# Relation products of a typed graph layer as eight 32-row products per tile on compact block-diagonal matrices, with staging and stores by whole tiles

## The chip, the cores and the metric

One core of one Trainium2 chip runs the whole program in one launch. The metric is the device time of the run in microseconds; the figure compared is the median of three runs.

## What is computed

Four graph layers run one after the other on 6250 nodes with 128 features and 100000 edges, each with a residual and a layer norm. The change lies ahead of the third one, a graph transformer with 8 heads of 16 columns, 8 node types and 8 edge types. Cut to what matters:

```python
k = _decomp(node_feat, node_type, w_comp_k, w_basis_k).reshape(n, H, DK)   # H = 8, DK = 16
q = _decomp(node_feat, node_type, w_comp_q, w_basis_q).reshape(n, H, DK)
v = _decomp(node_feat, node_type, w_comp_v, w_basis_v).reshape(n, H, DK)
kt = jnp.einsum('nhi,thij->tnhj', k, relation_att)[edge_type, src]
e = (q[dst] * kt).sum(-1) * relation_pri[edge_type] * scale
...
vt = jnp.einsum('nhi,thij->tnhj', v, relation_msg)[edge_type, src]
```

`_decomp` multiplies each node's features by four basis matrices and adds the four products with coefficients of the node's type. The two products over i are the relation products: for each of 8 edge types and each head, the 16 columns of that head by a 16x16 matrix.

## The kernel before, in words

Everything is float32. The nodes are cut into 49 tiles of 128 (`NT`), in 7 groups (`NG`) of 7 (`GT`). The stage in question makes, for each tile, a table of k and v under every edge type (`t3`, 8 edge types x 128 nodes x 256 columns, 1 MB for a tile), from which the next stage gathers rows by edge. The stage begins and ends at a barrier of all engines. The order of the work is written out by hand: each engine has its own program, `first` and `turn`, and semaphores tie them. Group 0 and group 6 are unrolled, groups 1 to 5 are a loop over a register, so that 35 of the 49 tiles run in the loop.

For tile n the engines do this:

- TensorE transposes the features (`features`, L2475) and ScalarE copies them out (`features_T`, L2529). TensorE multiplies them by the four bases of k, v and q, one 512-column product each (`typed`, L2482). ScalarE takes the first part of each (L2544), and VectorE adds the three others (`sums_of`, L2453).
- TensorE transposes k and v (`raise_kv`, L2490), and ScalarE copies them to SBUF (`lower_kv`, L2535).
- TensorE multiplies k and v by the relation matrices (`rows`, L2498). These are block-diagonal: `rel` is 128 rows by 8 types x 128 columns, and within a type only the 16x16 blocks of the heads are not zero. One call of `rows` makes a piece `z`, four of the eight types: two products of 512 columns (k by `att`, v by `msg`), into two banks of PSUM. There are two pieces a tile, in different banks, 2048 moving columns in all.
- ScalarE copies each piece to a staging buffer (`rows`, L2550; 1024 columns at once), and SyncE stores it, 512 KB, to `t3` (L2425). Seven staging buffers are used in turn.

TensorE's order in a turn is `raise_kv(n)`, `typed(n+1)`, `rows(n, 0)`, `features(n+2)`, `rows(n, 1)`. ScalarE's is `lower_kv(n)`, `typed(n+1)`, `rows(n, 0)`, `features_T(n+2)`, `features(n+3)`, `rows(n, 1)`. The transposed features and the transposed k and v share bank 0 of PSUM, and so `raise_kv` waits for the copy of the features that was started before it:

```python
pe.wait_ge(xt_sb, n + 1 + ahead_by)    # in raise_kv: features_T(n+1) has been copied out
need(pe, kv_out, 2 * n + z - 1)        # in rows: the same piece of the tile before is copied out
```

Of the kernel before, what the change touches and what calls it, by code (L numbers as in the profile page):

```python
# [9 lines left out]
ALU = mybir.AluOpType  # L10
ACT = mybir.ActivationFunctionType
# [80 lines left out]
def build(nc, t, out):  # L92
    ctx = ExitStack()
    with ctx:
# [662 lines left out]
        TYPED_AT = NODE_C_AT + NT * 4 * NB  # L757
        basis = {n: arena[:, o:o + NB * D] for n, o in (("a", 0), ("k", TYPED_AT), ("q", TYPED_AT + NB * D), ("v", TYPED_AT + 2 * NB * D))}
        REL_AT = TYPED_AT + 3 * NB * D
        rel = {n: arena[:, REL_AT + i * TN * D:REL_AT + (i + 1) * TN * D] for i, n in enumerate(("att", "msg"))}  # L760
        FREE_AT = REL_AT + 2 * TN * D
        acc_att = arena[:, AT_ACC:AT_ACC + NT * (D + H)]
        acc_gcn = arena[:, AT_ACC:AT_ACC + NP]
# [1002 lines left out]
        def attention_pass(which, idx, table, width, keep, tab, tab_w, head_last, Nodes=None):  # L1766
# [102 lines left out]
            with nc.Block() as block:  # L1869
# [7 lines left out]
                @block.sync  # L1877
                def _(sp):
                    def lows(n, k, b):
                        need(sp, oT_hot, n - 1)  # L1880
                        sp.dma_start(lo_b[:, b, :], lo_rows[bass.ds(n, 1), :].to_broadcast([P, 8 * P])).then_inc(lo_in[b], 16)

                    def reload(n, k, r):

                        b = r % 2
                        need(sp, mm, 2 * n - 2)
                        sp.wait_ge(spilled[r], 16 * k + 16)
                        sp.dma_start(m[:, b, :, 0:D], spill[bass.ds(n, 1)].rearrange("o p (c f) -> p (o c) f", f=D)).then_inc(back_in[b], 16)

                    def weights():  # L1890

                        for n in "akqv":
                            sp.dma_start(basis[n].rearrange("p (b o) -> p b o", b=NB), t["L2_gnn_w_basis_" + n].rearrange("b (i o) -> i b o", o=D)).then_inc(wt_in, 16)
                        for m, n in enumerate("kvqa"):
                            sp.dma_start(comp[:, :, m, :], t["L2_gnn_w_comp_" + n].partition_broadcast(P)).then_inc(wt_in, 16)
                        sp.dma_start(pri, t["L2_gnn_relation_pri"].rearrange("t h -> (t h)").partition_broadcast(P)).then_inc(wt_in, 16)
                        sp.wait_ge(wt_zero, 4)
                        sp.dma_start(nt_rows[0:NT - 1, :], t["node_type_8"][0:(NT - 1) * P].rearrange("(t p) -> t p", p=P)).then_inc(wt_in, 16)
                        sp.dma_start(nt_rows[NT - 1:NT, 0:LAST], t["node_type_8"][(NT - 1) * P:N].unsqueeze(0)).then_inc(wt_in, 16)
                        for n in ("att", "msg"):  # L1900
                            for h in range(H):
                                sp.dma_start(rel[n][h * DK:(h + 1) * DK, :].rearrange("p (t o) -> p t o", t=TN)[:, :, h * DK:(h + 1) * DK],
                                             t["L2_gnn_relation_" + n][:, h].rearrange("t i j -> i t j")).then_inc(wt_blk, 16)
# [228 lines left out]
                def _(dve):  # L2132
# [40 lines left out]
                    def priorities():  # L2173
                        step = Chain(dve, wt_v, 3 * TN)
                        dve.wait_ge(wt_blk, 16 * 2 * H)
                        step(nc.vector.tensor_scalar(pri, pri, DK ** -0.5, None, ALU.mult))
                        att = rel["att"].rearrange("p (c j) -> p c j", j=DK)
                        step(nc.vector.tensor_tensor(att, att, bcast_last(pri, DK), ALU.mult))

                    def messages(v, j, b):  # L2180

# [207 lines left out]
        new_stage()  # L2389
        x_rdy, xt_ps, xt_sb = (sem("n3_" + n) for n in ("x", "xtps", "xtsb"))  # L2390
        c_set, parts_ps, based, summed, kv_up, kv_sb, kv_ps, kv_out = (sem("n3_" + n) for n in ("cset", "parts", "based", "summed", "kvup", "kvsb", "kvps", "kvout"))
        kv_dma = [sem(f"n3_dma{i}") for i in range(GT)]
        x_new, xT = (scratch(AT_BUF + i * GC, GC) for i in range(1, 3))
        kv_T = scratch(AT_BUF + 3 * GC, 2 * GC).rearrange("p (t a n) -> p t a n", t=GT, a=2)
        KV_AT = FREE_AT
        kv_st = [scratch(AT_BUF + 5 * GC if i == 0 else KV_AT + (i - 1) * 1024, 1024).rearrange("p (t f) -> p t f", f=2 * D) for i in range(GT)]
        kvq = scratch(AT_BUF + 5 * GC + 1024, GT * 3 * D).rearrange("p (t m f) -> p t m f", t=GT, m=3)
        c_st = scratch(AT_BUF + 5 * GC + 1024 + GT * 3 * D, GT * 4 * NB)
        assert AT_BUF + 5 * GC + 1024 + GT * 3 * D + GT * 4 * NB <= EDGES_AT and KV_AT + (GT - 1) * 1024 <= 12800
        t3_rows = t3.rearrange("(t n) f -> n t f", t=TN)  # L2400
        PIECES = 2 * GT
        SUMS = 3 * (NB - 1)
        raised_ps, features_ps = ps[:, 0:2 * P], ps[:, 2 * P:3 * P]

        def part_bank(m):
            return (5 + m) * 512

        def piece_banks(z):
            return ps[:, (1 + 2 * z) * 512:(3 + 2 * z) * 512].rearrange("p (a c) -> p a c", a=2)

        def of_node(i, m, b):
            at_c = 4 * NB * i + NB * m + b
# [4 lines left out]
        with nc.Block() as block:  # L2417
            @block.sync
            def _(sp):
                def body(k):  # L2420
                    for i, number in enumerate(numbers(sp, GT * k, GT)):
                        for z in range(2):
                            n = PIECES * k + 2 * i + z
                            sp.wait_ge(kv_out, n + 1)
                            sp.dma_start(t3_rows[bass.ds(P * number, P), 4 * z:4 * z + 4, :], kv_st[(2 * i + z) % GT]).then_inc(kv_dma[(2 * i + z) % GT], 16)  # L2425
                turns(sp, NG, body)
                for i in range(GT):
                    sp.wait_ge(kv_dma[i], 16 * 2 * NG)

            @block.gpsimd  # L2430
            def _(pool):
# [37 lines left out]
            def _(pe):  # L2469
# [20 lines left out]
                        last = nc.tensor.transpose(raised_ps[:, m * P:(m + 1) * P], kvq[:, i, m], ident[:, :])  # L2490
                    last.then_inc(kv_up, 1)

                def rows(k, i, z):
                    n = GT * k + i
                    pe.wait_ge(kv_sb, n + 1)
                    need(pe, kv_out, 2 * n + z - 1)
                    for a, name in enumerate(("att", "msg")):
                        last = nc.tensor.matmul(piece_banks(z)[:, a, :], kv_T[:, i, a], rel[name][:, z * 512:(z + 1) * 512], start=True, stop=True)  # L2498
                    last.then_inc(kv_ps, 1)

                def first(k):
                    features(k, 0)
# [3 lines left out]
                def turn(k, more):  # L2506
                    for i in range(GT):
                        raise_kv(k, i, 1 if more or i + 1 < GT else 0)
                        if more or i + 1 < GT:
                            typed(*tile_at(k, i + 1))  # L2510
                        rows(k, i, 0)
                        if more or i + 2 < GT:
                            features(*tile_at(k, i + 2))
                        rows(k, i, 1)
                ahead(pe, first, turn)

            @block.scalar
            def _(act):
# [12 lines left out]
                def lower_kv(k, i):  # L2531
                    n = GT * k + i
                    act.wait_ge(kv_up, n + 1)
                    need(act, kv_ps, 2 * (n - GT) + 2)
                    nc.scalar.activation(kv_T[:, i], raised_ps.rearrange("p (a n) -> p a n", a=2), ACT.Copy).then_inc(kv_sb, 1)  # L2535

                def typed(k, i):
# [5 lines left out]
                        act.wait_ge(parts_ps, 3 * n + m + 1)  # L2543
                        nc.scalar.activation(kvq[:, i, m], ps[:, part_bank(m):part_bank(m) + D], ACT.Copy, scale=of_node(i, m, 0)).then_inc(based, 1)  # L2544

                def rows(k, i, z):
                    p = 2 * i + z
                    act.wait_ge(kv_ps, PIECES * k + p + 1)
                    need(act, kv_dma[p % GT], 16 * (2 * k + p // GT))
                    nc.scalar.activation(kv_st[p % GT].rearrange("p t (a f) -> p a t f", a=2),  # L2550
                                         piece_banks(z).rearrange("p a (t f) -> p a t f", f=D), ACT.Copy).then_inc(kv_out, 1)

                def first(k):
                    features(k, 0)
# [6 lines left out]
                def turn(k, more):  # L2561
                    for i in range(GT):
                        lower_kv(k, i)
                        if more or i + 1 < GT:
                            typed(*tile_at(k, i + 1))
                        rows(k, i, 0)
                        if more or i + 2 < GT:
                            features_T(*tile_at(k, i + 2))
                        if more or i + 3 < GT:
                            features(*tile_at(k, i + 3))  # L2570
                        rows(k, i, 1)
                ahead(act, first, turn)

        attention_pass("hgt", d_typed, t3, 2 * D, D, q_tab, D, False)
# [450 lines left out]
```

## Time and profile before

| | before |
|---|---|
| median of 3 runs | 9756.16 us (9746.25 to 9768.41) |
| span of the profiled execution | 7728.3 us |
| TensorE busy | 5090.6 us, 66% |
| VectorE busy | 4789.3 us, 62% |
| ScalarE busy | 3333.2 us, 43% |
| GpSimd busy | 4957.0 us, 64% |
| mean granted TensorE clock | 0.773 |
| the stage in question | about 4762 to 5084 us of the span |

The profile was taken in one execution. Its span goes from the first to the last instruction; of this execution only the span is given, and the median of the runs is 2027.9 us longer than it. A time in the trace is counted from the start of the span. "PEclk" is the granted clock of TensorE as a share of the full 2.4 GHz. A float32 product of TensorE stands in the trace as two weight loads and two products ("MATMUL"), a transpose as one.

### The profile page before, as it was taken

The numbers are of one execution on the slowest core, as the hardware profiler recorded it, in microseconds if no ns is written. First come the engines' busy times: TensorE is split into PE (matmuls) and PEld (weight loads), VectorE is DVE, ScalarE is ACT, GpSimd is POOL, SyncE is SP. The second block draws the span as 40 slices with busy tenths as digits, with TensorE's granted clock in tenths as the row PEclk, the third lists the DMA queues.
The fourth block names the chain that finished last, engine by engine and source line by source line (L and its number), as shares of the span: only waits on it lengthen the run. The fifth ranks groups of instructions, "written<-read, shape, count | busy, mean of one in ns | idle before, by whom it ended". The sixth has DMA issues, their size and how long they took to land. (4 is left out here: it accounts for less than half of the span.)

```text
span 7728.3 us, 120435 instructions
## 1 busy us (share of the span) xinstructions
PE 5090.6 (66%) x26514; PEld 3820.1 (49%) x26515; DVE 4789.3 (62%) x13170; ACT 3333.2 (43%) x8012; POOL 4957.0 (64%) x4968
## 2 busy tenths in 40 slices
PE   8777775666675777772555556956666565777674
PEld 6655653444444555551444444435555543555453
DVE  8766665555554677774566665436666565665666
ACT  0222221444444455540444445536666542555553
POOL 0677775777776777774777770057777601777774
PEclk9655566888887888885666667977777787999997
DMA  0222221111213112123666664467777812666665
GB/s 27 62 54 53 55 52 49 53 55 55 54 54 47 53 54 55 54 54 86 181 176 179 178 174 99 164 182 226 223 225 228 207 58 103 199 198 200 198 199 141
DMA packets 818131, 920.95 MB, mean 119 GB/s; under 512 B 120930, under 2 KB 657002, under 8 KB 817706
## 3 DMA queue, kind: packets, MB, share of 16 engines
q0 software_dynamic: 198144, 441.54, 22.0%
q1 hardware_dynamic: 395902, 365.44, 15.8%
q10 hardware_dynamic: 223916, 112.15, 5.0%
q8 instruction: 54, 0.88, 0.0%
q14 instruction: 115, 0.94, 0.0%
HBM read 724.85 MB, written 193.87 MB: 119 GB/s over the span
## 5 line engine op out<-in xcount | busy, mean ns | idle before, releaser
L788 POOL DMA_INDIRECT arena<-t,stage_idx x3328 | 3288.2, 988 | 1484.5 <-issue 989.7
L827 PE MATMUL ps<-arena 128*128 128x128 f32 (+2 forms) x8320 | 1786.1, 375 | 768.6 <-DMA arena<-t,stage_idx 624.0
L827 PEld LDWEIGHTS ps<-arena 128*128 128x128 f32 x8320 | 1569.0, 256 | 1033.1 <-issue 938.2
L836 DVE TENSOR_TENSOR arena<-arena,ps 128x512 f32 (+2 forms) x1040 | 834.9, 803 | 668.9 <-PE ps L827 610.8
L744 POOL DMA_INDIRECT d_rec<-arena x784 | 787.8, 1005 | 440.6 <-issue 242.3
L2832 POOL DMA_INDIRECT arena<-t,stage_idx x832 | 841.6, 1012 | 296.8 <-issue 222.1
L824 PE MATMUL ps<-int_tmp 128*128 128x512 bf16 (+1 forms) x1664 | 549.9, 399 | 601.8 <-DVE arena L836 327.6
L1279 PE MATMUL ps<-arena 128*128 128x416 f16 x3328 | 736.3, 373 | 0.0
L2042 PE MATMUL ps<-arena 128*128 x2496 | 393.3, 293 | 435.8 <-ACT arena L1930 248.7
L1211 ACT ACTIVATE arena<-arena 128x128 f16<-128x128 f16 x1664 | 662.2, 480 | 6.9
L2042 PEld LDWEIGHTS ps<-arena 128*128 128x128 f32 (+1 forms) x2496 | 343.5, 201 | 496.1 <-issue 473.5
L1938 ACT ACTIVATE arena<-iota_row,stage_lw 128x128 f32<-128x128 f32 x1664 | 508.7, 388 | 6.8
L824 PEld LDWEIGHTS ps<-int_tmp 128*128 128x128 bf16 x1664 | 149.3, 110 | 726.5 <-DVE arena L836 405.9
L1236 DVE TENSOR_SCALAR arena<-iota_row,stage_lw 128x128 f32<-128x128 f32 x1664 | 474.9, 365 | 53.5 <-DVE stage_lw L1228 49.2
L705 PE MATMUL ps<-arena 128*128 128x49 f32 x1568 | 328.0, 391 | 249.7 <-DVE arena L596 249.4
L705 PEld LDWEIGHTS ps<-arena 128*128 128x128 f32 x1568 | 319.8, 310 | 291.1 <-issue 224.6
L2865 ACT ACTIVATE arena<-iota_row,small 128x128 f32<-128x128 f32 x832 | 254.6, 388 | 466.0 <-PE ps L827 465.7
L1279 PEld LDWEIGHTS ps<-arena 128*128 128x128 f16 x3328 | 322.3, 110 | 228.9 <-issue 77.0
L2929 DVE TENSOR_TENSOR arena<-ps,arena 128x512 f32<-128x512 f32 x208 | 143.8, 692 | 452.2 <-DMA arena<-t,stage_idx 394.2
L2294 DVE TENSOR_TENSOR arena<-ps,arena 128x512 f32<-128x512 f32 x208 | 135.6, 687 | 333.6 <-DMA arena<-t,stage_idx 287.1
L1247 DVE TENSOR_SCALAR arena<-arena 128x832 f16<-128x832 f16 x832 | 316.9, 441 | 0.0
L2194 DVE TENSOR_TENSOR arena<-arena 128x512 f32<-128x512 f32 x416 | 268.3, 686 | 39.6 <-DMA arena<-spill 35.0
(466 smaller groups left out, 8299.9 us busy)
## 6 DMA issues: line engine op xcount, KB each, us to landing
spill<-arena ACTq DMA_DIRECT2D x208, 512.0 KB, 4.2
arena<-spill SPq DMA_DIRECT2D x208, 512.0 KB
arena<-t,stage_idx POOLq DMA_INDIRECT x4160, 3.2
arena<-d_loT SPq DMA_DIRECT2D x208, 256.0 KB
arena<-s_loT SPq DMA_DIRECT2D x104, 512.0 KB, 4.2
arena<-key_d SPq DMA_DIRECT2D x98, 512.0 KB
t<-arena SPq DMA_DIRECT2D x98, 512.0 KB, 2.9
d_rec<-arena POOLq DMA_INDIRECT x784
```

Of the source, the lines that this page charges most:

```text
L705: last = nc.tensor.matmul(pick_bank(b)[:, i * NT:(i + 1) * NT], at_loT[:, b, i * EC:(i + 1) * EC], run, start=True, stop=True)
L744: pool.indirect_dma_start(out=d_rec[:, :], out_offset=bass.IndirectOffsetOnAxis(ap=row[:, 8 * b + i:8 * b + i + 1], axis=0), in_=recs_st[: ...
L788: pool.indirect_dma_start(out=rows[r][:, i, :], out_offset=None, in_=table, in_offset=bass.IndirectOffsetOnAxis(ap=stage_idx[:, 8 * r + i: ...
L824: nc.tensor.matmul(half[:, :, 0:self.width], zeros16[:, 0:P], self.blank, start=True, stop=False, skip_group_check=True)
L827: return nc.tensor.matmul(self.banks[i // 4][:, bass.ds(self.slot[i], self.width)], weights, rows, start=False, stop=False, skip_group_che ...
L836: nc.vector.tensor_tensor(at, at, got, ALU.add).then_inc(self.added, 1)
L1211: last = nc.scalar.activation(at_r[:, b, a, j], far[:, b, j], ACT.Relu, bias=place_st[:, b, 2 + 2 * a, j:j + 1], scale=place_st[:, b, 3 + ...
L1236: one_hot = nc.vector.tensor_scalar(at[:, s, :], iota_row[:, :], lw_st[:, s, 0:1], lw_st[:, s, 1:2], ALU.is_equal, ALU.mult)
L1279: nc.tensor.matmul(place_bank(a, z), at_r[:, b, a, j], at_q[:, b, j, z * Q_W:(z + 1) * Q_W], start=False, stop=False, skip_group_check=True)
L1938: last = nc.scalar.activation(at[:, b, i], iota_row[:, :], ACT.Abs, bias=minus_lo[:, 8 * b + i:8 * b + i + 1])
L2042: last = nc.tensor.matmul(looked_up(b, z)[:, (i - 4 * z) * tab_w:(i - 4 * z + 1) * tab_w], hot_T[:, b, i * P:(i + 1) * P], source[:, bass. ...
L2832: pool.indirect_dma_start(out=rows[:, i, :], out_offset=None, in_=t4, in_offset=bass.IndirectOffsetOnAxis(ap=stage_idx[:, i:i + 1], axis=0 ...
```

## The change

The relation matrices are kept compact. Heads 2g and 2g+1 lie in the 32 partitions of group g, and for each type only the 32 columns of these two heads are kept, so `rel` is 128 rows by 8 types x 32 columns. A tile's products are now eight: for k, then for v, and for each of four groups of 32 partitions, the 32 rows of that group by 256 columns. Each group writes a bank of its own, k in one half and v in the other. ScalarE copies group by group, 512 columns each, into a staging buffer that holds a whole tile (three of them, 1 MB each, chosen by (k + i) mod 3), and SyncE stores a whole tile with one transfer. `features` and `features_T` now come behind the whole of `rows`.

```diff
-        rel = {n: arena[:, REL_AT + i * TN * D:REL_AT + (i + 1) * TN * D] for i, n in enumerate(("att", "msg"))}
+        GROUPS_OF = P // 32
+        REL_W = TN * 32
+        rel = {n: arena[:, REL_AT + i * REL_W:REL_AT + (i + 1) * REL_W] for i, n in enumerate(("att", "msg"))}
...
-                        att = rel["att"].rearrange("p (c j) -> p c j", j=DK)
-                        step(nc.vector.tensor_tensor(att, att, bcast_last(pri, DK), ALU.mult))
+                        two = 32 // DK
+                        for g in range(GROUPS_OF):
+                            of_g = slice(32 * g, 32 * g + 32)
...
+                            step(nc.vector.tensor_tensor(att, att, bcast_last(pri_g, DK), ALU.mult))
...
+        STAGES = 3
...
+        def kv_st(k, i):
+
+            return arena[:, bass.ds(KV_AT + ST_W * ((k + i) % STAGES), ST_W)].rearrange("p (t f) -> p t f", f=2 * D)
...
-                        for z in range(2):
-                            n = PIECES * k + 2 * i + z
-                            sp.wait_ge(kv_out, n + 1)
-                            sp.dma_start(t3_rows[bass.ds(P * number, P), 4 * z:4 * z + 4, :], kv_st[(2 * i + z) % GT]).then_inc(kv_dma[(2 * i + z) % GT], 16)
+                        sp.wait_ge(kv_out, GROUPS_OF * (GT * k + i + 1))
+                        sp.dma_start(t3_rows[bass.ds(P * number, P), :, :], kv_st(k, i)).then_inc(kv_dma[i], 16)
...
-                def rows(k, i, z):
+                def rows(k, i):
                     n = GT * k + i
                     pe.wait_ge(kv_sb, n + 1)
-                    need(pe, kv_out, 2 * n + z - 1)
+                    need(pe, kv_out, GROUPS_OF * n)
                     for a, name in enumerate(("att", "msg")):
-                        last = nc.tensor.matmul(piece_banks(z)[:, a, :], kv_T[:, i, a], rel[name][:, z * 512:(z + 1) * 512], start=True, stop=True)
-                    last.then_inc(kv_ps, 1)
+                        for g in range(GROUPS_OF):
+                            of_g = slice(32 * g, 32 * g + 32)
+                            last = nc.tensor.matmul(group_bank(g)[:, a, :], kv_T[of_g, i, a], rel[name][of_g, :], start=True, stop=True)
+                            if a == 1:
+                                last.then_inc(kv_ps, 1)
...
-                        rows(k, i, 0)
+                        rows(k, i)
                         if more or i + 2 < GT:
                             features(*tile_at(k, i + 2))
-                        rows(k, i, 1)
...
-                def rows(k, i, z):
-                    p = 2 * i + z
-                    act.wait_ge(kv_ps, PIECES * k + p + 1)
-                    need(act, kv_dma[p % GT], 16 * (2 * k + p // GT))
-                    nc.scalar.activation(kv_st[p % GT].rearrange("p t (a f) -> p a t f", a=2),
-                                         piece_banks(z).rearrange("p a (t f) -> p a t f", f=D), ACT.Copy).then_inc(kv_out, 1)
+                def rows(k, i):
+                    n = GT * k + i
+                    need(act, kv_dma[(i - STAGES) % GT], 16 * (k + (i >= STAGES)))
+                    for g in range(GROUPS_OF):
+                        act.wait_ge(kv_ps, GROUPS_OF * n + g + 1)
+                        of_g = kv_st(k, i).rearrange("p t (a g f) -> p a t g f", a=2, g=GROUPS_OF)[:, :, :, g, :]
+                        nc.scalar.activation(of_g, group_bank(g).rearrange("p a (t f) -> p a t f", t=TN), ACT.Copy).then_inc(kv_out, 1)
...
-                        rows(k, i, 0)
+                        rows(k, i)
                         if more or i + 2 < GT:
                             features_T(*tile_at(k, i + 2))
                         if more or i + 3 < GT:
                             features(*tile_at(k, i + 3))
-                        rows(k, i, 1)
```

How the instructions of TensorE stand in group 0 of the stage, one tile and the start of the next, before (L2490 is `raise_kv`, L2482 `typed`, L2498 `rows`, L2475 `features`):

```order
L2490 MATMUL ps<-ident,arena 128x128 x2
L2482 MATMUL ps<-arena 128x512 x3
L2498 MATMUL ps<-arena 128x512 x2
L2475 MATMUL ps<-ident,arena 128x128
L2498 MATMUL ps<-arena 128x512 x2
L2490 MATMUL ps<-ident,arena 128x128 x2
L2482 MATMUL ps<-arena 128x512 x3
```

And now (L2499 is `raise_kv`, L2491 `typed`, L2509 `rows`, L2484 `features`):

```order
L2499 MATMUL ps<-ident,arena 128x128 x2
L2491 MATMUL ps<-arena 128x512 x3
L2509 MATMUL ps<-arena 128x256 x8
L2484 MATMUL ps<-ident,arena 128x128
L2499 MATMUL ps<-ident,arena 128x128 x2
L2491 MATMUL ps<-arena 128x512 x3
```

The four 512-column products have become eight of 256 columns in one run, and the transpose of the features has moved from between the two pieces to behind all eight.

ScalarE in the unrolled group 0 before, one tile (L2535 is `lower_kv`, L2544 `typed`, L2550 `rows`, L2529 `features_T`, L2523 `features`):

```order
L2535 ACTIVATE arena<-ps 128x256
L2544 ACTIVATE arena<-ps,arena 128x128 x3
L2550 ACTIVATE arena<-ps 128x2x4x128
L2529 ACTIVATE arena<-ps 128x128
L2523 ACTIVATE arena<-x_cur 128x128
L2550 ACTIVATE arena<-ps 128x2x4x128
```

And now, in the loop, the end of one tile (L2563 is `rows`, L2540 `features_T`, L2534 `features`, L2546 `lower_kv`; "ISA" and "REGISTER_ALU" work out addresses and counts in registers):

```order
L2561 REGISTER_ALU
L2563 ISA
L2563 ACTIVATE arena<-ps 128x2x8x32
L2538 REGISTER_ALU
L80 ISA
L2540 ACTIVATE arena<-ps 128x128
L80 ISA
L2534 ISA
L2534 ACTIVATE arena<-x_cur 128x128
L80 ISA
L2546 ACTIVATE arena<-ps 128x256
```

`features_T`, which stood between the two copies of a tile, now stands behind the last of four, and each of these has register work of its own ahead of it.

## Rows read from the trace of the kernel before

**Rows 1.** The page: span, and busy time of the engines.
```profile
span 7728.3 us, 120435 instructions
PE 5090.6 (66%) x26514; PEld 3820.1 (49%) x26515; DVE 4789.3 (62%) x13170; ACT 3333.2 (43%) x8012; POOL 4957.0 (64%) x4968
```
**Rows 2.** Windows in the stage: busy of PE, PEld, DVE, ACT, POOL; PEclk, DMA share, GB/s.
```profile
4800.00:4850.00 50.00, 50.00 (x135) 22.84 (x134) 24.39 (x79) 29.07 (x64) 0.00 (x0) 1.00 0.48 169
4950.00:5000.00 50.00, 50.00 (x136) 22.88 (x135) 24.48 (x79) 29.06 (x64) 0.00 (x0) 1.00 0.46 164
```
**Rows 3.** Groups of instructions by form, 4775 to 5080 us.
```profile
L2498 PE MATMUL ps<-arena 128*128 128x512 f32 x387 | 179.3, 593 | 1.2 <-ACT arena L2535 1.2
L2550 ACT ACTIVATE arena<-ps 128x1024 f32<-128x1024 f32 x98 | 100.3, 1023 | 89.5 <-PE ps L2498 89.5
```
**Rows 4.** Timeline of one tile in the loop: start, us, engine, line, operation, idle before.
```profile
4901.61 0.35 DVE L2453 SCALAR_TENSOR_TENSOR arena<-ps,arena 128x128 f32 x1 [0.21 <-DVE arena L2453]
...
4902.03 0.27 ACT L2529 ACTIVATE arena<-ps 128x128 f32<-128x128 f32 x1
4902.35 0.14 PEld L2490 LDWEIGHTS ps<-ident,arena 128*128 128x128 f32 x1 [0.28 <-ACT arena L2529]
...
4902.94 1.02 ACT L2550 ACTIVATE arena<-ps 128x1024 f32<-128x1024 f32 x1 [0.44 <-PE ps L2498]
4902.95 2.74 PE L2482 MATMUL ps<-arena 128*128 128x512 f32 x6
...
4903.85 0.38 ACT L2535 ACTIVATE arena<-ps 128x256 f32<-128x256 f32 x1
...
4904.59 3.15 DVE L2453 SCALAR_TENSOR_TENSOR arena<-ps,arena 128x128 f32<-128x128 f32 x8 [2.08 <-ACT arena L2544]
...
4905.53 1.88 PE L2498 MATMUL ps<-arena 128*128 128x512 f32 x4
...
4907.53 1.02 ACT L2550 ACTIVATE arena<-ps 128x1024 f32<-128x1024 f32 x1 [1.43 <-PE ps L2498]
...
4909.30 2.74 PE L2482 MATMUL ps<-arena 128*128 128x512 f32 x6
```
**Rows 5.** Timeline: the first tile, where TensorE started from idle.
```profile
4763.95 5.26 PE L2482 MATMUL ps<-arena 128*128 128x512 f32 x6
...
4769.40 0.44 PE L2490 MATMUL ps<-ident,arena 128*128 128x128 f32 x2 [0.18 <-DVE arena L2453]
4769.68 0.59 PE L2482 MATMUL ps<-arena 128*128 128x512 f32 x1
```
**Rows 6.** Timeline of TensorE in a later stage, full products and one-row products.
```profile
6491.15 1.72 PE L915 MATMUL ps<-l_T,arena 128*128 128x128 f32 x14
6492.71 1.73 PE L915 MATMUL ps<-w_sb,arena 128*128 128x128 f32 x14
6494.36 1.82 PE L2689 MATMUL ps<-bias_sb,ones 1*128 1x128 f32 x14
```
**Rows 7.** ScalarE's 512-column copies out of PSUM in other stages.
```profile
L1962 ACT ACTIVATE arena<-ps 128x512 f32<-128x512 f32 x26 | 15.6, 598 | 116.0 <-PE ps L2029 116.0
```
**Rows 8.** The stage's end: the last copy and the next stage's first transfer.
```profile
5079.11 1.02 ACT L2550 ACTIVATE arena<-ps 128x1024 f32<-128x1024 f32 x1 [0.69 <-PE ps L2498]
5084.30 0.37 SPq L1881 DMA_DIRECT2D arena<-d_loT  x1
```
**Rows 9.** The clears and the scaling of the relation matrices, each by its line.
```profile
L2149 DVE MEMSET arena<- x1: 912/912/912, 3565.0 to 3565.0; 128x1024 f32 x1
L2178 DVE TENSOR_TENSOR arena<-arena x1: 1224/1224/1224, 3661.4 to 3661.4; 128x1024 f32<-128x1024 f32 x1
```
**Rows 10.** Windows of a later stage: PE busy, PEclk, DMA share, GB/s.
```profile
6332.00:6336.00 4.00, 2.15 (x5) 1.00 0.00 0
6344.00:6348.00 4.00, 1.80 (x15) 1.00 0.00 0
6348.00:6352.00 4.00, 0.00 (x0) 0.67 0.80 291
```

More of the change, by code:

```diff
@@ L1901, in weights @@
                             for h in range(H):
-                                sp.dma_start(rel[n][h * DK:(h + 1) * DK, :].rearrange("p (t o) -> p t o", t=TN)[:, :, h * DK:(h + 1) * DK],
+                                lane = h * DK % 32
+                                sp.dma_start(rel[n][h * DK:(h + 1) * DK, :].rearrange("p (t o) -> p t o", t=TN)[:, :, lane:lane + DK],
                                              t["L2_gnn_relation_" + n][:, h].rearrange("t i j -> i t j")).then_inc(wt_blk, 16)
@@ L2176, in priorities @@
                         step(nc.vector.tensor_scalar(pri, pri, DK ** -0.5, None, ALU.mult))
-                        att = rel["att"].rearrange("p (c j) -> p c j", j=DK)
-                        step(nc.vector.tensor_tensor(att, att, bcast_last(pri, DK), ALU.mult))
+                        two = 32 // DK
+                        for g in range(GROUPS_OF):
+                            of_g = slice(32 * g, 32 * g + 32)
+                            att = rel["att"][of_g].rearrange("p (t q j) -> p t q j", t=TN, j=DK)
+                            pri_g = pri[of_g].rearrange("p (t h) -> p t h", h=H)[:, :, two * g:two * g + two]
+                            step(nc.vector.tensor_tensor(att, att, bcast_last(pri_g, DK), ALU.mult))
                     def messages(v, j, b):
@@ L2395, in build, with group_bank @@
         KV_AT = FREE_AT
[L2396 to L2399, printed above, removed]
+        ST_W = TN * 2 * D
+        kvq = scratch(AT_BUF + 5 * GC, GT * 3 * D).rearrange("p (t m f) -> p t m f", t=GT, m=3)
+        c_st = scratch(AT_BUF + 5 * GC + GT * 3 * D, GT * 4 * NB)
+        assert AT_BUF + 5 * GC + GT * 3 * D + GT * 4 * NB <= EDGES_AT and KV_AT + STAGES * ST_W <= 12800 and GT % STAGES == 1
         t3_rows = t3.rearrange("(t n) f -> n t f", t=TN)
-        PIECES = 2 * GT
         SUMS = 3 * (NB - 1)
         raised_ps, features_ps = ps[:, 0:2 * P], ps[:, 2 * P:3 * P]
+        def kv_st(k, i):
+            return arena[:, bass.ds(KV_AT + ST_W * ((k + i) % STAGES), ST_W)].rearrange("p (t f) -> p t f", f=2 * D)
         def part_bank(m):
             return (5 + m) * 512
-        def piece_banks(z):
-            return ps[:, (1 + 2 * z) * 512:(3 + 2 * z) * 512].rearrange("p (a c) -> p a c", a=2)
+        def group_bank(g):
+            return ps[:, (1 + g) * 512:(2 + g) * 512].rearrange("p (a c) -> p a c", a=2)
         def of_node(i, m, b):
@@ L2421, in body @@
                     for i, number in enumerate(numbers(sp, GT * k, GT)):
-                        for z in range(2):
-                            n = PIECES * k + 2 * i + z
-                            sp.wait_ge(kv_out, n + 1)
-                            sp.dma_start(t3_rows[bass.ds(P * number, P), 4 * z:4 * z + 4, :], kv_st[(2 * i + z) % GT]).then_inc(kv_dma[(2 * i + z) % GT], 16)
+                        sp.wait_ge(kv_out, GROUPS_OF * (GT * k + i + 1))
+                        sp.dma_start(t3_rows[bass.ds(P * number, P), :, :], kv_st(k, i)).then_inc(kv_dma[i], 16)
                 turns(sp, NG, body)
                 for i in range(GT):
-                    sp.wait_ge(kv_dma[i], 16 * 2 * NG)
+                    sp.wait_ge(kv_dma[i], 16 * NG)
             @block.gpsimd
@@ L2533, in lower_kv @@
                     act.wait_ge(kv_up, n + 1)
-                    need(act, kv_ps, 2 * (n - GT) + 2)
+                    need(act, kv_ps, GROUPS_OF * (n - GT) + GROUPS_OF)
                     nc.scalar.activation(kv_T[:, i], raised_ps.rearrange("p (a n) -> p a n", a=2), ACT.Copy).then_inc(kv_sb, 1)
```

## The prediction

> **What bounds the kernel now.** I read the page first: no engine is busy for more than 66% of the span [rows 1], so nothing is to be read from the average, and the change touches one stage of some 310 us between two barriers. So I went to the windows of that stage. There TensorE is busy all the time, 50.00 of 50.00 us, at granted clock 1.00, with ScalarE at 29 and VectorE at 24 of 50, and the DMA engines at a share below 0.5 [rows 2]. Before the change TensorE sets the stage's pace. The groups say what ends ScalarE's waits: it waits 89.5 us for the relation products, and these wait 1.2 us for it [rows 3]. The timeline of one tile shows the period. The typed products start at 4902.95 and again at 4909.30: 6.35 us a tile [rows 4]. In it, the six records of the typed products take 4905.53 - 4902.95 = 2.58 us, 0.43 us a record of 512 columns (1.2 GHz would double that: six took 5.26 us in the first tile [rows 5]). The relation products are eight such records, 3.44 us; transposes fill the rest.
>
> **What the change does to this.** Moving columns stay at 2048 a tile: sixteen records of 256 columns, 0.43 / 2 = 0.215 us each, 3.44 us if they follow one another. A saving can only come from products of different partition groups running at the same time. What the change certainly does is in the order. `raise_kv(n+1)` waits for `features_T(n+2)`, which ScalarE now starts only behind all four copies of tile n. Before, that copy stood between the two pieces, and TensorE still had the second piece to do: the copy starts at 4902.03 and the weight load of `raise_kv` follows at 4902.35, behind running products [rows 4]. Now TensorE has nothing left. The period becomes a closed chain through both engines:
>
> 1. from the start of `raise_kv` to the first typed product, TensorE idle before: 4769.68 - 4769.40 = 0.28 us [rows 5];
> 2. the typed products: 2.58 us [rows 4];
> 3. the change from 128-row to 32-row products. Fourteen full products take 6492.71 - 6491.15 = 1.56 us, and the next fourteen, followed by one-row products, 6494.36 - 6492.71 = 1.65 us [rows 6]: 0.09 us;
> 4. relation products until group 0 of v is through, then the signal. In the trace ScalarE starts 4907.53 - 4905.53 = 2.00 us behind the first of four records, that is 4 x 0.43 + 0.28 [rows 4]. The first copy can start when the tenth record is through;
> 5. four copies of 512 columns. One lasts 598 ns [rows 7]; the next instruction starts 0.11 us before one ends (1.02 us for L2550 at 4902.94, L2535 at 4903.85 [rows 4]), so 0.49 us each, 1.96 us;
> 6. from the start of `features_T` to `raise_kv`: 4902.35 - 4902.03 = 0.32 us [rows 4];
> 7. in the loop the address of the copy is worked out behind the wait. VectorE's last sum, whose address is dynamic too, starts 0.21 us behind the one before [rows 4], where sums with fixed addresses stand about 0.04 apart (eight of 0.35 us in 3.15 us). I take 0.17 us once a tile; for the other copies it lies beside the copy before.
>
> Item 4 is the unknown. No row shows products of different 32-row groups side by side. **Upper bound:** no overlap: 10 x 0.215 + 0.28 = 2.43 us. **Lower bound:** the four groups run wholly together, and a round costs one product, 0.43 us: 2 x 0.43 + 0.28 = 1.14 us. In between: the two records of one product use the same rows and can't overlap, and records start in order; so the first record of group g+1 goes beside the second of group g, a new product starts every 0.215 us, and the tenth record is through after 6 x 0.215: 1.29 + 0.28 = 1.57 us. I take this one, since the records of a float32 product come in pairs and the code issues group behind group.
>
> Period with fixed addresses: 0.28 + 2.58 + 0.09 + 1.57 + 1.96 + 0.32 = 6.80 us, in the loop 6.97 us. Against 6.35 that is 0.45 us for 13 of the 48 periods and 0.62 us for 35: 5.9 + 21.7 = **+27.6 us**. TensorE's work falls to about 5 us a tile and is then idle for almost 2, waiting for ScalarE.
>
> The Trainium skill, TensorEngine Tiling (Array Packing), PSUM Bottleneck, says that packing speeds up TensorE but not the copies out of PSUM, which may become the bottleneck; and TensorE: Matmul & The Clock Gate, Part 3, gives a measured 3.07x for four row tiles of 512 columns. As an estimate by that figure the relation products take 3.44 / 3.07 = 1.12 us, item 4 becomes 1.40 us, and the sum +19 us in place of +27.6. No trace here shows that figure.
>
> The small edits: the stores carry the same bytes, a whole tile every 7 us into three buffers. A buffer is needed again some 18 us later; now seven half-size stores are in the ring and ScalarE never waits for one, and from the last copy (ends 5080.13) to the next stage's first transfer it is 4.17 us with 512 KB [rows 8]. That tail may grow by 1.5 us with 1 MB, or not at all if the engines share it better. One end less: group-wise copies let the last tile finish about 1 us earlier. The two clears of the relation matrices shrink from 912 ns to a quarter, 1.4 us less at the start of a stage; the scaling, 1224 ns, becomes four pieces [rows 9], about the same. I take -1 us for all, bounds -3 and +3. Sum: **+27 us**.
>
> **Profile and median.** The sum is made in the profiled execution, whose span is 7728.3 us; the median of the runs is 2027.9 us longer [rows 1]. No row says what fills that; I take it as the same before and after, so 9756 + 27 = 9783 us. Were it spread over the program, 27 would become 34. I count 0.2%, 19.5 us, as what a measurement of this kernel can tell from no change.
>
> **The rivals.**
>
> *No overlap of the groups.* Item 4 is 2.43 us, the period 7.66 and 7.83, and 13 x 1.31 + 35 x 1.48 - 1 = +68 us: 9824 us. For it: every product in the trace is paced by its columns, one behind the other. Against: the groups use different rows and different banks.
>
> *Full overlap.* Item 4 is 1.14 us, 0.43 us less: 27 - 48 x 0.43 = +6 us, 9762 us, no change that can be told. For it: the order k for all groups, then v for all, leaves each group free for three products. Against: the paired records. This is the case that the skill's Part 3, named above, speaks for; the Trainium skill's figure would put it at +19.
>
> *The clock falls.* TensorE is now idle for 2 of every 7 us. At 1.2 GHz the chain would be about 0.45 + 5.16 + 0.09 + 2.86 + 0.17 + 1.96 + 0.32 = 11.0 us, +223 us if all periods were so; a quarter of them gives about +80. For it: the clock falls to 0.67 in a window without work. Against: it stays at 1.00 through windows with 2.15 and 1.80 of 4 us [rows 10], and at 1.2 GHz TensorE would be busy again for 9 of 11 us. 9830 to 9980 us.
>
> *Faster.* The other side needs TensorE to be the slower party. If in the timed runs the clock of this stage were lower than the 1.00 of the profile, the work taken from TensorE would weigh more: before, a tile costs 6.35 / f; after, about 4.15 / f + 2.82. They cross at f = 0.78. At f = 0.5 it is 12.7 against 11.1, 49 x 1.6 = 78 us less: 9680 us. For it: the unexplained 2 ms between span and median, and the mean clock of 0.773. Against: [rows 2] at 1.00.
>
> **How the numbers follow.** Half overlap 0.49 (9772 to 9800, of which some 0.06 lies below the 0.2% line), no overlap 0.21 (9810 to 9845), full overlap 0.12, falling clock 0.08, faster 0.10. Faster by over 0.2%: 0.10. Within 0.2%: 0.12 + 0.06 = 0.18. Slower: 0.43 + 0.21 + 0.08 = 0.72. The likeliest is 9783 us, its own range 9772 to 9800. The range for 8 in 10 leaves out faster (0.10) and most of the falling clock (0.08): 9755 to 9855 us.
>
> **What would show it.** In the windows of the stage TensorE's busy time falls from 50 to some 36 to 40 of 50 at clock 1.00. In the timeline the typed products start every 6.8 to 7.0 us; `raise_kv` (L2499) has about 1.9 us of idle ahead of it, ended by `features_T` (L2540). The relation products (L2509) show starts 0.1 to 0.12 us apart if they overlap by half, 0.215 if not. The four copies (L2563) last about 0.6 us each, back to back. I would be wrong if `raise_kv` found `features_T` done, if the copies of 32-column runs took another time than plain ones, or if a copy waited for a store.

## The result, and the profile after

The changed kernel takes 9793.73 us (median of 5 runs, 9782.37 to 9812.03) against 9757.12 us before (5 runs, 9746.25 to 9773.53): a ratio of 1.0037, 95% interval 1.0025 to 1.0049, or 24 to 48 us slower. The forecast was 9783.

The page after shows a span that does not answer to [rows 1]: 9780.5 us against 7728.3. The kernel before had been timed in executions of some 9757 us and profiled in one of some 7730 us, and the experiments show that it has both speeds. So the spans can't be compared here, only the stage itself.

```profile
span 9780.5 us, 121265 instructions
PE 5352.0 (55%) x26906; PEld 3939.9 (40%) x26907; DVE 4755.0 (49%) x13173; ACT 3321.8 (34%) x8110; POOL 4953.1 (51%) x4968
```

Windows of the stage after, to be set beside [rows 2] (busy of PE, PEld, DVE, ACT, POOL; PEclk, DMA share, GB/s):

```profile
6290.00:6340.00 50.00, 33.39 (x193) 16.16 (x192) 23.78 (x76) 28.51 (x73) 0.00 (x0) 0.97 0.45 157
6340.00:6390.00 50.00, 33.22 (x175) 15.95 (x175) 22.45 (x72) 28.25 (x73) 0.00 (x0) 0.93 0.42 147
```

TensorE's busy time has fallen from 50 to 33 us of 50, so products of different groups ran side by side. ScalarE still has 28 to 29. And the granted clock is no longer 1.00.

The timeline of one tile after, to be set beside [rows 4]:

```profile
6399.99 2.23 DVE L2462 SCALAR_TENSOR_TENSOR arena<-ps,arena 128x128 f32<-128x128 f32 x6
6400.22 0.74 PEld L2509 LDWEIGHTS ps<-arena 32*128 32x128 f32 x16 [0.76 <-issue]
6400.22 1.15 PE L2509 MATMUL ps<-arena 32*128 32x256 f32 x16
6400.33 0.37 ACT L2555 ACTIVATE arena<-ps,arena 128x128 f32<-128x128 f32 x1 [0.49 <-PE ps L2491]
6401.30 0.14 PEld L2484 LDWEIGHTS ps<-ident,arena 128*128 128x128 f32 x1 [0.33 <-issue]
6401.30 0.33 PE L2484 MATMUL ps<-ident,arena 128*128 128x128 f32 x1
6401.54 2.06 ACT L2563 ACTIVATE arena<-ps 128x512 f32 x4 [0.85 <-PE ps L2509]
...
6403.47 0.31 ACT L2540 ACTIVATE arena<-ps 128x128 f32<-128x128 f32 x1
...
6403.89 0.20 PEld L2499 LDWEIGHTS ps<-ident,arena 128*128 128x128 f32 x2 [2.46 <-issue]
6403.92 0.41 PE L2499 MATMUL ps<-ident,arena 128*128 128x128 f32 x2 [2.29 <-ACT arena L2540]
...
6404.17 2.74 PE L2491 MATMUL ps<-arena 128*128 128x512 f32 x6
...
6406.84 1.15 PE L2509 MATMUL ps<-arena 32*128 32x256 f32 x16
```

Read it as a round. The sixteen records of the relation products start at 6400.22 and take 1.15 us, where eight of 512 columns took 3.44. ScalarE's four copies start at 6401.54, its copy of the features at 6403.47, `raise_kv` at 6403.89, the typed products at 6404.17, and the next relation products at 6406.84: 6.62 us a tile, against 6.35. `raise_kv` has 2.29 us of idle ahead of it, ended by L2540. Over the whole stage, too, most of the idle time ahead of `raise_kv` is ended by this copy:

```profile
L2499 PE MATMUL ps<-ident,arena x98: 272/299/477, 6238.7 to 6565.6; 128*128 128x128 f32 x98
...
  ACT arena L2540: 129.5, 57
```

From the first load of features to the next stage's first transfer it is 6576.80 - 6231.66 = 345.1 us, before 5084.30 - 4762.41 = 321.9 us: 23.2 us more. The first loads, before and after:

```profile
4762.41 0.51 ACT L2523 ACTIVATE arena<-x_cur 128x128 f32<-128x128 f32 x2 [3.15 <-PEq L107]
```
```profile
6231.66 0.51 ACT L2534 ACTIVATE arena<-x_cur 128x128 f32<-128x128 f32 x2 [3.16 <-PEq L107]
```

And the stage's end, beside [rows 8]:

```profile
6568.90 2.06 ACT L2563 ACTIVATE arena<-ps 128x512 f32<-128x512 f32 x4 [1.28 <-PE ps L2509]
6576.80 0.85 SPq L1883 DMA_DIRECT2D arena<-d_loT  x2
```

The last copy ends at 6570.96, and the barrier opens 5.84 us later; before it was 4.17.

### The profile page after: what moved, and what is told of

It reads as the page before. It is cut to its first block and busy times, and to the rows that moved or that the text cites. A ratio compares the mean times of both kernels' runs of the same rounds, so it can differ in the third digit from the quotient of the medians.

```text
span 9780.5 us, 121265 instructions
## 1 busy us (share of the span) xinstructions
PE 5352.0 (55%) x26906; PEld 3939.9 (40%) x26907; DVE 4755.0 (49%) x13173; ACT 3321.8 (34%) x8110; POOL 4953.1 (51%) x4968
## 5 line engine op out<-in xcount | busy, mean ns | idle before, releaser
L829 PE MATMUL ps<-arena 128*128 128x128 f32 (+2 forms) x8320 | 1851.4, 378 | 351.0 <-issue 279.8
L829 PEld LDWEIGHTS ps<-arena 128*128 128x128 f32 x8320 | 1630.2, 259 | 593.5 <-issue 483.0
L826 PE MATMUL ps<-int_tmp 128*128 128x512 bf16 (+1 forms) x1664 | 589.6, 424 | 1336.2 <-issue 692.3
L1281 PE MATMUL ps<-arena 128*128 128x416 f16 x3328 | 846.1, 382 | 540.8 <-issue 539.3
L2045 PE MATMUL ps<-arena 128*128 x2496 | 396.0, 299 | 510.0 <-issue 167.2
L705 PEld LDWEIGHTS ps<-arena 128*128 128x128 f32 x1568 | 334.9, 324 | 521.3 <-issue 519.4
L2940 DVE TENSOR_TENSOR arena<-ps,arena 128x512 f32<-128x512 f32 x208 | 143.3, 689 | 474.1 <-DMA arena<-t,stage_idx 261.1
L2894 PE MATMUL ps<-arena 128*128 x1664 | 278.1, 323 | 136.6 <-issue 135.7
L2894 PEld LDWEIGHTS ps<-arena 128*128 128x128 f32 x1664 | 258.1, 233 | 172.5 <-issue 167.9
L577 ACT ACTIVATE arena<-arena 128x392 bf16<-128x392 bf16 x98 | 89.8, 916 | 648.7 <-DVE arena L342 420.8
```

The costliest lines, as they stand in the source:

```text
L705: last = nc.tensor.matmul(pick_bank(b)[:, i * NT:(i + 1) * NT], at_loT[:, b, i * EC:(i + 1) * EC], run, start=True, stop=True)
L826: nc.tensor.matmul(half[:, :, 0:self.width], zeros16[:, 0:P], self.blank, start=True, stop=False, skip_group_check=True)
L829: return nc.tensor.matmul(self.banks[i // 4][:, bass.ds(self.slot[i], self.width)], weights, rows, start=False, stop=False, skip_group_che ...
L1281: nc.tensor.matmul(place_bank(a, z), at_r[:, b, a, j], at_q[:, b, j, z * Q_W:(z + 1) * Q_W], start=False, stop=False, skip_group_check=True)
L2045: last = nc.tensor.matmul(looked_up(b, z)[:, (i - 4 * z) * tab_w:(i - 4 * z + 1) * tab_w], hot_T[:, b, i * P:(i + 1) * P], source[:, bass. ...
L2894: last = nc.tensor.matmul(ps[:, o_ps:o_ps + D], hot_T[:, b, i * P:(i + 1) * P], p_tab[:, bass.ds(tiles[i] * D, D)], start=True, stop=True)
```

## The experiments

Eleven kernels were run in three batches, each beside the kernel before on one chip. Below, "stage" is the time from the start of the first relation product to the start of the last in the profile: 306.1 us before, 326.8 us in the changed kernel.

```profile
L2498 PE MATMUL ps<-arena x392: 592/592/697, 4772.4 to 5078.5; 128*128 128x512 f32 x196
```
```profile
L2509 PE MATMUL ps<-arena x784: 374/374/479, 6241.6 to 6568.4; 32*128 32x256 f32 x196
```

**The kernel before, again.**

> The kernel before, unchanged, under a new name. It gives a second profile of it, since the first has a span 2027.9 us shorter than its runs while the profile after has a span of 9780.5 us. If something in that one trace was left out, this span comes out near 9755 us and the stage again at 322 us (4762.4 to 5084.3 before); if the kernel really has two speeds, it may come out near 7730 us again. The ratio should be 1.000 within 0.2%.

Median 7745.57 us, ratio 1.0002 (0.9992 to 1.0012), span 7743.7, stage 306.1 us. So the kernel has two speeds: here it takes 7745 us, in the third batch 7744, in the second 9650, and beside the runs of the result it took 9757. Within a batch it keeps to one of them (9609 to 9665 us in 21 runs of the second). Nothing was left out of the first trace; the guess of a gap in it was wrong. The second batch and the third both ran on a chip with the number 7, so the runs don't show that the speed belongs to the chip. The windows of the first graph stage show where the time differs, here first in this run, then in the result's profile of the changed kernel, whose work there is the same:

```profile
1700.00:2000.00 300.00, 202.53 (x1113) 152.36 (x1112) 168.78 (x542) 140.38 (x392) 228.38 (x236) 0.83 0.22 54
```
```profile
1700.00:2000.00 300.00, 158.32 (x836) 105.42 (x836) 123.22 (x403) 104.73 (x292) 186.29 (x187) 0.69 0.15 43
```

GpSimd issues 236 gathers in 300 us at one speed and 187 at the other, and the DMA engines move 54 and 43 GB/s. All stages that gather or scatter are longer in the slower launches. Why was not tried. The stage of this change has the same length in the changed kernel at both speeds (345.1, 343.4 and 345.1 us from end to end at spans of 9780.5, 9665.9 and 7746.5). Of the kernel before there are traces at the faster speed only, 321.9 and 322.0 us.

**The features back between the copies.**

```diff
-                        rows(k, i)
+                        rows(k, i, (0, 1))
                         if more or i + 2 < GT:
                             features_T(*tile_at(k, i + 2))
                         if more or i + 3 < GT:
                             features(*tile_at(k, i + 3))
+                        rows(k, i, (2, 3))
```

> The changed kernel, but ScalarE copies the transposed features (and loads the next ones) between the second and third of its four copies, where the place was before; nothing else moves. Theory A (the chain through features_T sets the pace): raise_kv can start two copies, 0.97 us, earlier in every tile, the period falls from 6.62 us (6.86 with the stretches at the lower clock) to about 5.65 us, and the run is some 45 to 60 us faster than the changed kernel, 15 to 25 us faster than before. Rival B (the four smaller copies themselves, or their register work, set the pace of ScalarE): ScalarE has the same work, so nothing moves, within 10 us of the changed kernel.

7698.49 us, ratio 0.9939 (0.9922 to 0.9955) to before, 47 us faster; the stage is 267.9 us, 58.9 less than in the changed kernel. ScalarE's work is the same, so theory B falls. The expectation from the periods, 45 to 60 less than the changed kernel, held for the stage: two copies, 0.97 us, in 47 periods are 45.6 us, and the clock, which no longer falls, gives the other 13 (see the run with TensorE kept busy). Against before it is more than the 15 to 25 that I gave.

```profile
4850.00:4900.00 50.00, 38.99 (x225) 18.83 (x225) 27.82 (x90) 33.50 (x90) 0.00 (x0) 1.00 0.53 186
```

The clock is back at 1.00, with 39 us of work in 50 and 1.3 us of idle ahead of `raise_kv`.

**The features ahead of the products.** The diff shows TensorE's turn; on ScalarE `features_T` and `features` move ahead of `rows` in the same way.

```diff
-                        rows(k, i)
                         if more or i + 2 < GT:
                             features(*tile_at(k, i + 2))
+                        rows(k, i)
```

> The changed kernel, but the transpose of the features stands ahead of the eight products on TensorE and its copy ahead of the four copies on ScalarE. Theory A: the chain through the copies is cut; the next bound is the round through ScalarE's typed copies and VectorE's sums, about 4.8 to 5.0 us a tile, so some 85 to 100 us faster than the changed kernel and 50 to 70 us faster than before. Rival B: no change beyond 10 us.

7666.4 us, ratio 0.9897 (0.988 to 0.9914), 79 us faster than before, where I had expected 50 to 70; stage 229.5 us, 4.78 us a tile on the mean. The run at the end of this section repeats it beside the changed kernel.

```profile
4903.81 2.06 ACT L2563 ACTIVATE arena<-ps 128x512 f32 x4 [0.57 <-PE ps L2509]
4904.44 0.43 PE L2499 MATMUL ps<-ident,arena 128*128 128x128 f32 x2 [0.80 <-DVE arena L2462]
...
4905.73 0.42 ACT L2546 ACTIVATE arena<-ps 128x256 f32<-128x256 f32 x1
4905.99 0.41 ACT L2555 ACTIVATE arena<-ps,arena 128x128 f32<-128x128 f32 x1
```

`raise_kv` no longer waits for ScalarE's copies: it starts beside them, when VectorE's sums are done. But the copies still hold something up. The first typed copy (L2555), from which the next sums begin, comes right behind them.

**The order alone, in the kernel before**, on TensorE as shown and on ScalarE in the same way.

```diff
                         rows(k, i, 0)
+                        rows(k, i, 1)
                         if more or i + 2 < GT:
                             features(*tile_at(k, i + 2))
-                        rows(k, i, 1)
```

> The kernel before, with the full 512-column products and two pieces, but the transpose of the features and its copy moved behind the second piece, as the change has them. It prices this part alone. Theory A: period 0.28 + 2.58 + 3.44 + 0.28 + 0.91 + 0.42 = 7.91 us against 6.35, so 75 us slower than before, up to 90 if the clock falls in the gaps. Rival B (the products alone set the pace, and the place of the transpose costs nothing): 0 to +10 us.

7810.94 us, ratio 1.0087 (1.0071 to 1.0104), 66 us slower, where theory A had 75; stage 374.2 us, clock 1.00. The period is 7.79 us, where it had 7.91:

```profile
4901.41 2.74 PE L2482 MATMUL ps<-arena 128*128 128x512 f32 x6
...
4903.99 3.60 PE L2498 MATMUL ps<-arena 128*128 128x512 f32 x8
...
4907.62 1.02 ACT L2550 ACTIVATE arena<-ps 128x1024 f32<-128x1024 f32 x1 [0.69 <-PE ps L2498]
4908.54 0.27 ACT L2529 ACTIVATE arena<-ps 128x128 f32<-128x128 f32 x1
...
4908.96 0.41 PE L2490 MATMUL ps<-ident,arena 128*128 128x128 f32 x2 [1.26 <-ACT arena L2529]
4909.20 1.02 PE L2482 MATMUL ps<-arena 128*128 128x512 f32 x2
```

Nothing of the products has changed here, only the place of one transpose, its copy and the load behind it, and TensorE now waits for ScalarE. This is the part of the change that costs.

**The changed kernel, again, in the second batch.**

> The changed kernel, unchanged, under a new name, beside the kernel before on one chip. The times differ by a quarter between chips (9757 us and 7745 us for the kernel before), so the change is to be priced where the other kernels were. The two traces so far, from two chips, show a period of 6.62 us with the clock at 1.00 and 6.86 on the mean against 6.35 before, and a stage of 345.1 us against 321.9. If the stage is all there is to it, this run is 20 to 27 us slower than before on this chip too; if the 36 us measured on the slower chip come from elsewhere too, 30 us or more.

9667.72 us against 9649.57, ratio 1.0024 (1.0014 to 1.0034), 23 us slower (14 to 33) by the ratio, 18 by the medians, where 20 to 27 was expected; stage 325.1 us.

**No overlap.** All products on 128 rows: `kv_T[:, i, a]` and `rel[name]` in place of `kv_T[of_g, i, a]` and `rel[name][of_g, :]`.

> The changed kernel with all eight products on 128 rows (each then sums over all four groups, so the table holds other values): same columns, same banks, same copies, but no product can run beside another. Theory: the relation products take 3.44 us in place of 1.15, the first copy starts after 10 x 0.215 + 0.28 = 2.43 us in place of 1.32 us, the period is 7.6 us, 38 to 53 us slower than the changed kernel by periods (1.1 less the clock's 0.24 us at best). Rival: if the copies hide the products, nothing changes.

9725.64 us, ratio 1.0084 (1.0067 to 1.01). The stage is 369.1 us, 44 more than in the changed kernel beside it, within the 38 to 53 expected; the medians differ by 58. The products take three times as long:

```profile
6303.32 3.62 PE L2509 MATMUL ps<-arena 128*128 128x256 f32 x16
...
6305.84 2.06 ACT L2563 ACTIVATE arena<-ps 128x512 f32 x4 [1.95 <-PE ps L2509]
```

**TensorE kept busy.** Behind the eight products of each tile:

```diff
+                    for _ in range(6):
+                        nc.tensor.matmul(ps[:, 3 * P:4 * P], kv_T[:, i, 0], rel["att"][:, 0:P], start=True, stop=True)
```

> The changed kernel with six more products a tile (128 columns of the compact matrix into an unused part of bank 0, never read) behind the eight, in TensorE's idle stretch of 2.3 us, which they shorten to about 1 us. Theory: the mean period of 6.86 us against 6.62 at full clock comes from stretches in which the granted clock falls because of this idle time; with it shortened the windows of the stage read 1.00 and the run is 5 to 12 us faster than the changed kernel in spite of more work. Rival: the clock's dips have another cause, and it is the same within 3 us or slower.

9654.48 us against 9667.72 for the changed kernel. The ratios to before, 1.0017 (1.0003 to 1.0031) and 1.0024 (1.0014 to 1.0034), overlap, so the run times don't settle it. The stage does: 313.4 us against 325.1, and the clock is 1.00 in every window read.

```profile
6300.00:6350.00 50.00, 43.81 (x289) 26.23 (x288) 24.50 (x78) 29.27 (x75) 0.00 (x0) 1.00 0.48 166
```

More work on TensorE made the stage 11.7 us shorter. The two stages:

```profile
L2509 PE MATMUL ps<-arena x784: 374/374/478, 6174.4 to 6499.5; 32*128 32x256 f32 x196
```
```profile
L2509 PE MATMUL ps<-arena x784: 374/374/478, 6150.7 to 6464.1; 32*128 32x256 f32 x196
```

What it took away is this, in the changed kernel of the same batch (PE busy, PEclk, DMA share, GB/s):

```profile
6304.00:6306.00 2.00, 1.02 (x17) 1.00 0.35 116
6306.00:6308.00 2.00, 0.78 (x3) 0.72 0.00 0
6308.00:6310.00 2.00, 2.00 (x3) 0.50 0.85 301
6310.00:6312.00 2.00, 2.00 (x12) 0.93 0.66 223
```
```profile
6307.70 4.03 PE L2491 MATMUL ps<-arena 128*128 128x512 f32 x6
```

Behind some of the idle stretches the clock falls to 1.2 GHz, for the typed products of one tile: their six records take 4.03 us in place of 2.74, and the tile 7.84 us in place of 6.62. Over the whole stage, 8 of the 48 periods of this run, from one tile's first relation product to the next one's, last 7.9 us or more, 9 in the result's profile and in the third batch, and none in the run with more work. That is 11.7 / 8 = 1.5 us for each, and 326.8 - 313.4 = 13.4 us for the nine of the result.

**The loops exchanged** (`for g` outside, `for a` inside).

> The changed kernel with the two loops of the eight products exchanged: k and v of group 0, then k and v of group 1, and so on. My step of the prediction said that records of one group block the next in order. If TensorE starts records strictly in order, the four records of one group run one behind the other and only the last overlaps the next group's first: the first copy starts after 4 x 0.215 + 0.28 = 1.14 us, but the others come 0.65 us apart, and the period grows by some 0.4 us, 15 to 25 us slower than the changed kernel. If each group has its own queue, the order costs nothing, and the first copy comes earlier: 0 to -10 us.

9679.01 us, ratio 1.0034 (1.0021 to 1.0046); stage 325.2 us, as in the changed kernel (325.1). The products take 1.17 us, and the first copy still starts 1.33 us behind them:

```profile
6304.85 1.17 PE L2509 MATMUL ps<-arena 32*128 32x256 f32 x16
...
6306.18 2.06 ACT L2563 ACTIVATE arena<-ps 128x512 f32 x4 [0.85 <-PE ps L2509]
```

The second outcome came, for the stage: the order costs nothing (the medians differ by 11 us, the stage by 0.1). So records do not start in the order of the program. In that order a group's four records, 0.215 us apart, would stand ahead of the next group's, and the sixteen would take about 3 us, as an estimate from these 0.215 us; they took 1.17. In the trace they start in four rounds of four, at 0, 0.32, 0.54 and 0.75 us, with this order of the loops and with the other, and each round spans 0.04 us at most. The first copy doesn't come earlier, as I had thought it might, and it had no reason to: a group's own four records follow one another in either order, and the last round ends 1.13 us behind the first start.

**Features ahead, but no overlap.**

> The version with the features ahead of the eight products, but with all eight on 128 rows (each sums over all four groups, so the table holds other values). It asks whether that version gained by its order alone. Theory: without overlap TensorE has 0.28 + 2.58 + 0.11 + 3.44 us of work a tile, 6.4 us, and sets the pace again: within 10 us of the kernel before, so all of the gain of 79 us needs the overlap. Rival: the order alone gives the gain, and this kernel is 50 us or more faster than before.

7737.38 us, ratio 0.999 (0.998 to 0.9999). TensorE sets the pace again, 6.36 us a tile (typed products at 4902.73 and 4909.09). The order alone only takes back what the order cost; all of the gain needs the overlap as well. The four stages side by side: no overlap, features behind 369.1 us and ahead 307.0; with overlap, behind 326.8 and ahead 229.5.

**Features ahead, and the changed kernel, in one batch.**

> The version with the features ahead, again, beside the changed kernel on one chip: 70 to 85 us faster than before, and 95 to 105 us faster than the changed kernel.

> The changed kernel a third time, to have its price on the chip of the other two. The traces give 21 to 23 us for the stage whatever the chip, and the two measurements so far 36 us (24 to 48) and 23 us (14 to 33). If the stage is all, 20 to 25 us slower than before.

Features ahead: 7661.3 us, ratio 0.9885 (0.987 to 0.99). Changed kernel: 7758.63 us, ratio 1.0017 (1.0008 to 1.0026), 6 to 20 us slower, at the lower edge of the 20 to 25 expected or below it, and 97 us behind the other. Its stage is 326.7 us, the longer one as in the result's profile. So three measurements of the change give 36, 23 and 13 us around a stage that is 19 to 21 us longer between its products in each, and 21 to 23 us longer from end to end. The difference must lie outside the stage. In the eight traces at the faster speed the stage begins anywhere from 4756.0 to 4777.2 us, whatever the kernel, so such amounts come and go ahead of it; no part of them was tied to the change.

## Why the prediction was right

It was right in the direction, and in the mechanism: a closed chain through ScalarE's copy of the features. That the time came so close, 9783 against 9793.73, is in part luck. The stage grew by 23.2 us where I had 27, but of these only 11.0 are the longer chain that I had at 27.6; a falling clock, which I had left out, gave 13.4. And the three measurements of the same change are 36, 23 and 13 us, the last with an interval that does not reach 27.

- **The closed chain.** Shown. `raise_kv` waits for `features_T`, and the place of that copy alone is worth +66 us in the kernel before, and -58.9 us of the stage when it is put back between the copies in the changed one, of which some 13 are the clock.
- **Items 1, 2, 3 and 5:** 0.28 us, 2.58 + 0.09 = 2.67 us (6406.84 - 6404.17), and 1.93 us for four copies where I had 1.96. All as forecast. The same stretch is 2.58 us in the run without overlap, so the 0.09 does belong to the change from 128-row to 32-row products.
- **Item 4, the step that failed.** I took a half overlap, 1.57 us, because I let records start in order, so that a new product starts every 0.215 us. Measured in the loop are 1.32 us, in which item 7 is contained; in the unrolled tiles, with fixed addresses, it is 1.16 us for the first three (6242.80 - 6241.64) and 1.22 us for the others. That is the lower bound of full overlap, 1.14, within 0.1 us. The four groups run side by side, and a group's record doesn't wait for the second record of another group's product. In the runs, sixteen records take 1.15 us side by side and 3.62 us one behind the other, a factor of 3.15. The Trainium skill, TensorE: Matmul & The Clock Gate, Part 3, has 3.07 for four row tiles of 512 columns; the trace, with 256 columns in float32, agrees.
- **Item 7:** between 1.32 - 1.22 = 0.10 and 1.32 - 1.16 = 0.16 us, forecast 0.17.
- **Item 6** was read where TensorE was still at work. With TensorE idle it is 0.42 us (6403.89 - 6403.47, and 4908.96 - 4908.54 in the order alone), not 0.32.
- **The sum.** With the clock at 1.00 the mean period grows from 6.34 to 6.58 us, 11.0 us in 47 periods. Before, the stage of 306.1 us less 5.0 for the last period, which is shorter, and 3.1 for the last tile's own products is 298.0; in the run with TensorE kept busy 313.4 less 3.6 and 0.8 is 309.0. I had 27.6 for 48. By itself this is nearer the rival of full overlap (+6) than my own.
- **The clock** filled the gap. I made it a rival at 0.08 and left it out of the sum. It fell in every trace of the changed kernel, in 9 of 48 periods of the result's profile, for 13.4 us of the stage. I had priced a slow period at 11.0 us, as if the whole round ran at the lower clock. It lasted 8.0 to 8.2, since the typed products alone did. I had read [rows 10] as saying that 2 us of idle in 4 are harmless. They don't show a pattern of 2.2 us of idle in every 6.6; the runs do: with 2.2 to 2.3 us of idle ahead of `raise_kv` the clock falls now and then, with 1.3 us (two orders), 1.2 us (no overlap) and 0.9 us it never did between the first relation product and the last `raise_kv`.
- **The ends.** The tail of 4.17 us became 5.84 us with a last store of 1 MB, 1.7 us more; all runs with 1 MB show 5.8. The bound of 1.5 was about right. The last tile takes 2.8 us less than before, where I had about 1: 1.4 in its period (3.62 us for 4.98) and 1.4 from its first product to the end of its last copy. In all 11.0 + 13.4 + 1.7 - 2.8 = 23.3 us, the 23.2 of the stage.
- **The signs.** `raise_kv` waits for `features_T` and the copies last 0.6 us back to back, as forecast. TensorE is busy for 33 us of 50, not 36 to 40, the period is 6.6 us, not 6.8 to 7.0, and the idle time 2.3 us, not 1.9: all three on the side of full overlap. No copy waited for a store.
- **The median against the span.** I took the 2027.9 us between them as time around the program. It was the other of the two speeds. The rival built on it, a lower clock of this stage in the timed runs, falls: the changed kernel's stage reads the same at both. So the sum needed no stretching to 34 either.

The Trainium skill, TensorEngine Tiling (Array Packing), PSUM Bottleneck, warns that after the speedup the copies out of PSUM may become the bound. The trace agrees that they came onto the path, but not by their amount: ScalarE is busy for 28 us of 50. They are on it by their place in the order: with the features ahead ScalarE is busy for more of the time, 38 us of 50, and `raise_kv` does not wait for it.

## What to carry to other kernels

When products are made cheaper, look at what the engine will wait for once they are gone: here it was one small copy that had always been ready because there were products left to do. A piece of work that others wait for goes ahead of the bulk of its engine's work, not behind it. And watch idle time of TensorE that comes back in every tile: here the clock that fell behind it cost 13.4 us, more than the 11.0 of the longer periods.

## What was not expected of the hardware

- The same kernel takes 7745, 9650 or 9757 us from one batch of runs to another; the difference is in the stages that gather or scatter (54 against 43 GB/s in the windows read), and none of it in this stage. The cause stays open.
- The float32 products of four 32-row groups run side by side almost without loss (1.15 us for sixteen records of 256 columns, 3.62 us one behind the other), in either order of the loops, so records of different groups do not start in the order of the program.
- Changing from 128-row to 32-row products costs 0.09 us (2.67 us against 2.58 without the change).
- Added products that nobody reads made a stage 11.7 us shorter, since they kept the clock at 2.4 GHz.
